# Fetching an expert block's rows in quarters of 512 bytes and transposing them on VectorE, in a fused attention and expert layer on one Trainium2 core

## The reference

```python
# B=32 batches, S=256 positions, 512 channels, 16 heads of 32, 8 expert tiles
x = x + attention(layernorm(x), ctx, ctx, Wq, Wk, Wv, Wo, masks)   # softmax over 256 masked keys
idx = argmax(pe @ sign(tile_sigs).T, axis=-1)                      # one expert for each position s
h   = layernorm(x)
x   = x + (h[b, s] @ W[idx[s]].T + b[idx[s]])                      # each row uses its position's expert
```

## Time and profile before

| | |
|---|---|
| median of 3 runs | 952.63 us (950.9 to 953.97) |
| the profiled execution, its own time | 953.35 us |
| its span, first to last instruction | 951.4 us |
| TensorE busy | 908.4 us (95%) |
| VectorE, GpSimd, ScalarE busy | 735.2, 567.1, 383.9 us |
| mean granted TensorE clock | 0.981 of 2.4 GHz |

### The profile page before, as it was taken

The page is one execution under the profiler, slowest core; times in us unless marked ns, Lnnn a source line. Parts: engine busy times, 40 slices in busy tenths (PEclk is TensorE's granted clock), DMA queues, the critical chain, the costliest instruction groups (busy, mean ns, idle before and its releaser), DMA issues.

```text
span 951.4 us, 16646 instructions
## 1 busy us (share of the span) xinstructions
PE 908.4 (95%) x5696; PEld 729.2 (77%) x5697; DVE 735.2 (77%) x1097; ACT 383.9 (40%) x697; POOL 567.1 (60%) x763
## 2 busy tenths in 40 slices
PE   5899999999999999999999999999739999999997
PEld 4687887887888788788878878887627888888885
DVE  5988867777776877877787787779758777777775
ACT  5554444454544445454444545444451111111110
POOL 3855746465574646557464654743645777777773
PEclk9999999999999999999999999999878999999999
DMA  9613133131313314131331313113643544444551
GB/s 336 225 72 102 56 113 91 60 121 46 104 53 113 101 53 117 45 110 48 113 102 56 113 45 113 52 51 117 224 142 112 158 161 162 163 158 159 162 164 50
DMA packets 48876, 108.10 MB, mean 114 GB/s; under 512 B 10496, under 2 KB 15136, under 8 KB 46624
## 3 DMA queue, kind: packets, MB, share of 16 engines
q1 hardware_dynamic: 37216, 71.70, 23.7%
q0 software_dynamic: 11200, 35.21, 11.6%
q10 hardware_dynamic: 384, 0.21, 0.1%
HBM read 73.47 MB, written 35.19 MB: 114 GB/s over the span
## 4 chain that ended last, share of the span: by engine, by line
PE 91%; DVE 3%; POOL 2%; DMA 1%; issue 1%; ACT 0%; SPq 0%; DVEq 0%; POOLq 0%
PE pS L1358 27%; PE pA L1652 21%; PE pA L1358 20%; PE pS L1416 7%; PE pA L1439 7%; PE pT L1427 6%; PE pT L1632 3%; PE pS L1384 1%; DMA x_scratch<-y 1%; POOL xt_lo L982 1%; POOL wo_lo L1030 0%; DMA wk_raw<-in_wk 0%; DMA xg<-x_scratch,gather_rows 0%; PE pT L1463 0%; DVE early L1312 0%
## 5 line engine op out<-in xcount | busy, mean ns | idle before, releaser
L1652 PE MATMUL pA<-wf_hl,x_hi 128*128 x560 | 183.3, 409 | 1.9 <-DVE x_lo L1586 1.9
L1203 DVE TENSOR_TENSOR s<-pS,bias 128x1024 f32<-128x1024 f32 x64 | 78.0, 1219 | 100.3 <-PE pS L1416 100.3
L998 POOL COPY y<-y_mom 128x1 f32<-128x1 f32 x64 | 12.9, 202 | 238.5 <-DVE y_mom L1242 238.5
L1015 POOL TENSOR_TENSOR s<-s,row 128x1024 f32<-128x1024 f32 x64 | 122.0, 1906 | 11.5 <-DVE row L1223 11.5
L1119 ACT CAST ot_hi<-pA 128x512 fp32r<-128x512 f32 x64 | 37.6, 588 | 222.6 <-PE pA L1439 222.6
L1546 POOL DMA_INDIRECT out_dram<-y,scatter_rows x70 | 94.1, 1344 | 54.4 <-DVE y L1594 52.8
L1565 ACT CAST x_hi<-pT 128x512 fp32r<-128x512 f32 x70 | 41.1, 587 | 191.0 <-PE pT L1632 159.1
L1652 PEld LDWEIGHTS pA<-wf_hl,x_hi 128*128 128x128 f32 x560 | 101.1, 191 | 21.2 <-issue 2.3
L1358 PE MATMUL pA<-wo_hi,ot_hi 128*128 128x512 f32 x256 | 109.2, 426 | 4.5 <-DVE ot_lo L1227 4.5
L1652 PE MATMUL pA<-wf_hl,x_lo 128*128 x280 | 111.5, 398 | 0.0
L1358 PE MATMUL pS<-xt_hi,wq_hi 128*128 128x512 f32 x256 | 105.6, 413 | 3.9 <-DVE wq_lo L1262 2.3
(11 more groups left out here) (124 smaller groups left out, 1898.9 us busy)
## 6 DMA issues: line engine op xcount, KB each, us to landing
x_scratch<-y SPq DMA_DIRECT2D x64, 257.0 KB, 3.0
xt_raw<-in_x_t SPq DMA_DIRECT2D x16, 1024.0 KB, 6.2
x<-in_x SPq DMA_DIRECT2D x64, 256.0 KB, 2.6
wf_hl<-in_wf SPq DMA_DIRECT2D x8, 1024.0 KB, 8.8
ctx_raw<-in_ctx_t SPq DMA_DIRECT2D x32, 128.0 KB, 3.1
bias_all<-in_bf SPq DMA_DIRECT2D x1, 2048.0 KB, 10.8
mask_early<-in_mask SPq DMA_DIRECT2D x1, 1536.0 KB, 11.6
xg<-x_scratch,gather_rows POOLq DMA_INDIRECT x70
```

What stands on the lines that cost most here:

```text
L1015: pool.tensor_tensor(p, p, h.row[:, t % h.c, 3, :].unsqueeze(2).broadcast_to([P, H, BK]), ALU.mult)\
L1203: dve.tensor_tensor(h.s_sb[:, t % h.c, :].rearrange("p (h k) -> p h k", h=H), pS[:, 0, :].rearrange("p (h k) -> p h k", h=H), h.bias[:, t ...
L1652: mm = pe.matmul(pA[:, r % 2, :], a[:, c * P:(c + 1) * P], w, start=(c == 0 and m == 0), stop=(c == KC - 1 and m == 2))
```

## The change

- Attention stores two things for each tile instead of one. `y_biased`, 128 rows of 2048 bytes: y plus the bias of its position's expert, by a GpSimd addition (`add_bias`). `y_normal`: the normalised rows, by a ScalarE activation (`y_normalise`), stored into a scratch `x_quarters` in which each quarter row (128 channels, 512 bytes) is a piece of its own.
- The two halves of the positions have their bias rows in `bias_at`, filled in the prologue by two indirect DMAs on GpSimd's queue, ahead of the low part of Wo. `bias_all` and its load go.
- In the expert stage GpSimd gathers only the biased rows. SyncE fetches the normalised ones, with one `value_load` and one DMA of 128 x 512 bytes for each of the block's four positions: 280 of each.
- These land with a quarter of the channels in each group of 32 partitions, so VectorE's transpose, which works in squares of 32x32, gives what the product needs (the expert weights' rows are reordered on the way in). TensorE's four transposes, VectorE's normalisation, its bias addition and its `value_load` go. The low part is now made from an SBUF tile and not from PSUM.

```diff
+        y_rows = nc.dram_tensor("y_scratch", (B * S, DM), F32, kind="Internal").ap()
+        x_quarters = nc.dram_tensor("x_scratch", (KC * B, S, P), F32, kind="Internal").ap()
...
+        def store_rows(sp, rows, batch, half, ring):
+            sp.dma_start(y_rows[rows, :], y_biased[:, ring, :]).then_inc(y_stored[ring], 16)
+            dst = x_quarters.rearrange("(i b) s f -> b s i f", i=KC)
+            sp.dma_start(dst[batch, half * P:(half + 1) * P] if isinstance(batch, int) else
+                         dst[batch, half * P:(half + 1) * P].rearrange("a s i f -> (a s) i f"),
+                         y_normal[:, ring, :].rearrange("p (i f) -> p i f", i=KC)).then_inc(y_stored[ring], 16)
...
             rstd(1)
+            pool.wait_ge(rv, MATCHED + 1)
+            for n in range(2):
+                pool.indirect_dma_start(bias_at[:, n, :], None, bf,
+                                        bass.IndirectOffsetOnAxis(ap=expert_at[:, n:n + 1], axis=0)).then_inc(bias_loaded, 16)
             pool.wait_ge(w_hi_ready["o"], 1)
...
+            def add_bias(t):
+                wait(pool, y_stored[t % 2], 32 * (t // 2))
+                pool.tensor_tensor(y_biased[:, t % 2, :], y_sb[:, t % 2, 0:DM], bias_at[:, t % 2, :], ALU.add)\
+                    .then_inc(y_biased_ready, 1)
...
+            def y_normalise(t):
+                y = y_sb[:, t % 2, :]
+                act.wait_ge(y_ready, t + 1)
+                wait(act, y_stored[t % 2], 32 * (t // 2))
+                act.activation(y_normal[:, t % 2, :], y[:, 0:DM], ACT.Identity, bias=y[:, DM:DM + 1],
+                               scale=y[:, DM + 1:DM + 2]).then_inc(y_normal_ready, 1)
...
+        def experts_sync(sp):
+            def gather_quarters(j):
+                r = j % R
+                wait(sp, x2t_ready, j + 1 - R)
+                for n in range(PB):
+                    s = sp.value_load(gather_rows[n * B:n * B + 1, j:j + 1], min_val=0, max_val=S - 1)
+                    sp.dma_start(xq[:, r, n * P:(n + 1) * P],
+                                 x_quarters[:, bass.ds(s, 1), :].rearrange("p a f -> p (a f)")).then_inc(quartered[r], 16)
+
+            for j in range(NR):
+                gather_quarters(j)
...
-                pool.indirect_dma_start(xg[:, r, :], None, x1,
+                pool.indirect_dma_start(yg[:, r, :], None, y_rows,
...
-                act.wait_ge(x2t_done, j + 1)
+                act.wait_ge(x2t_ready, j + 1)
                 wait(act, f_done, j - 1)
-                act.copy(x2_hi[:, j % 2, :], pT[:, j % 2, :]).then_inc(x2_hi_ready, 1)
+                act.copy(x2_hi[:, j % 2, :], x2t[:, j % 2, :]).then_inc(x2_hi_ready, 1)
...
+            def transpose(j):
                 r = j % R
-                wait(dve, x2t_done, j - 1)
-                dve.wait_ge(gathered[r], 16 * (j // R) + 16)
-                dve.tensor_scalar(xn2[:, j % 2, :], xg[:, r, 0:DM], xg[:, r, DM:DM + 1], xg[:, r, DM + 1:DM + 2],
-                                  ALU.subtract, ALU.mult).then_inc(xn2_ready, 1)
+                dve.wait_ge(quartered[r], 16 * PB * (j // R) + 16 * PB)
+                wait(dve, x2_lo_ready, j - 1)
+                dve.transpose(x2t[:, j % 2, :].rearrange("p (c g b) -> p c g b", c=KC, g=PB),
+                              xq[:, r, :].rearrange("p (g c a) -> p c g a", g=PB, c=KC)).then_inc(x2t_ready, 1)
...
             def body(k, n):
-                first = isinstance(k, int) and R * k + n == 0
-                if first:
-                    transpose(k, n + 1)
-                if is_block(k, n):
-                    e = expert(k, n)
-                if is_block(k, n + 1) and not first:
-                    transpose(k, n + 1)
-                if is_block(k, n):
-                    product(k, n, e)
+                product(k, n, expert(k, n))
```

More of the change, by code:

```diff
@@ L282, in kernel_program @@
         wf_loaded = [sem(f"wf_loaded_{t}") for t in range(NE)]
-        wf_hi_ready = [sem(f"wf_hi_ready_{t}") for t in range(NE)]
+        wf_hi_ready = sem("wf_hi_ready")
+        HIGH_ORDER = (0, 1, 2, 4, 5, 6, 7, 3)
         wf_lo_pool = sem("wf_lo_pool")
@@ L1057, in tiles @@
                 y_rstd(h.tiles - 2)
+                add_bias(h.tiles - 2)
                 y_rstd(h.tiles - 1)
+                add_bias(h.tiles - 1)
             return tiles
@@ L1182, in tiles @@
                         q_copy(g + 2, 0)
+                    if t >= 2:
+                        y_normalise(t - 2)
                     if t == h.tiles - 2:
                         expert_high(act, 1)
-                for t in (4, 5, 6, 7, 3):
+                y_normalise(h.tiles - 2)
+                expert_high(act, 4)
+                y_normalise(h.tiles - 1)
+                for t in (5, 6, 7, 3):
                     expert_high(act, t)
@@ L1522, in kernel_program @@
         y2 = sb("y2", [P, 3, DM])
-        xb_ready = sem("xb_ready")
         gathered = [sem(f"gathered_{r}") for r in range(R)]
-        xn2_ready = sem("xn2_ready")
-        x2t_done = sem("x2t_done")
+        quartered = [sem(f"quartered_{r}") for r in range(R)]
+        x2t_ready = sem("x2t_ready")
         x2_hi_ready = sem("x2_hi_ready")
@@ L1531, in kernel_program @@
         y2_ready = sem("y2_ready")
-        scattered = [sem(f"scattered_{r}") for r in range(R)]
+        scattered = [sem(f"scattered_{r}") for r in range(3)]
+        def experts_sync(sp):
[8 more added lines that the diff above has]
+                gather_quarters(j)
         def experts_gpsimd(pool):
@@ L1610, in experts_vector @@
                 if j + 2 < NR:
-                    normalise(j + 2)
+                    transpose(j + 2)
                 if j == 0:
@@ L1615, in experts_vector @@
                 finish(j)
-                if j + 1 < NR:
-                    add_bias(j + 1)
         def experts_tensor(pe):
             def at(k, n):
-                return R * k + n, n % R, k + n // R
-            def is_block(k, n):
-                return not isinstance(k, int) or 0 <= R * k + n < NR
-            def transpose(k, n):
-                j, r, turn = at(k, n)
-                pe.wait_ge(xn2_ready, j + 1)
-                wait(pe, x2_lo_ready, j - 1)
-                for c in range(KC):
-                    mm = pe.transpose(pT[:, r % 2, c * P:(c + 1) * P], xn2[:, r % 2, c * P:(c + 1) * P], ident[:])
-                mm.then_inc(x2t_done, 1)
+                return R * k + n, n % R
             def expert(k, n):
-                j, r, turn = at(k, n)
+                j, r = at(k, n)
                 e = pe.value_load(expert_of[0:1, bass.ds(j, 1)], min_val=0, max_val=NE - 1)
@@ L1672, in experts_tensor @@
                     body(k, n)
-            for n in range(NR + 1 - R * turns):
+            for n in range(NR - R * turns):
                 body(turns, n)
```

123 lines of the change are left out of this document (66 added, 57 removed).

## The result

The changed kernel takes 1090.91 us (median of 4, 1090.76 to 1091.67), the kernel before 952.98 us beside it: a ratio of 1.1452, 95% interval 1.1432 to 1.1472, so 14.5% slower. The forecast was 1069 us with a range of 1008 to 1125. The profiled execution has a span of 1089.9 us, against 951.4 before.

The account below looks back on a forecast made before the run. TensorE was taken to bound both stages, with SyncE pacing the changed expert stage: quarters start at 710.5, plus 342.3 us to the last issue at 1052.8, then the tail, a span of 1067.4; forecast 1069 us, range 1008 to 1125.

Parts of the forecast that it names:

- SyncE paces the stage: Expert stage: SyncE's loads and issues take 4.89 us per block (3.97 to 6.7), above the product's 2.80; chance 0.82.
- the rival with the DMA engines as the bound: Expert stage: DMA engines need 4.9 us per block, 1070 us in all, with a DMA share near 1; chance 0.04.
- 1.21 us for a quarter: Expert stage: SyncE's register load, bounds check, address, DMA issue and gaps for one position, between 0.98 and 1.66 us.
- TensorE's 30.8 us: Expert stage: 70 blocks without four transposes of 0.44 us in all save TensorE 30.8 us, which turn into idle time.
- TensorE busy for about 57%: Expert stage: TensorE works 2.80 us of each 4.89 us block, with a granted clock below 1.
- Start of the quarters, 710.5: Change-over to the expert stage: SyncE's quarters start at 710.5 us, 4.2 us later than the gathers' start before.
- The prologue: Two bias gathers in GpSimd's chain ahead of Wo's low part cost 3.2 us on the path, between 2.3 and 4.7.
- Attention, costed at nothing: Attention: GpSimd's addition, ScalarE's activation and the second store hide under TensorE's 100%; without that cover 98 us.
- The change-over: Attention to expert stage: stores start at about 705 us, behind the last expert's weights, which load 3.2 us later.
- The tail: After the last issue: landing 2.6, transpose 0.8, rounding 0.6, low part 0.9, product 2.8, then 6.9 us to the end.
- The clock: Expert stage: TensorE's clock goes up and down at little cost; rival staying at 1.2 GHz, about 1086 us, chance 0.04.
- The DMA share: Expert stage: a DMA share of about 0.5 to 0.6, against 0.49 before.

Follow-up runs that it names:

- e1: The changed kernel without its 280 register loads, SyncE issuing the same 280 DMAs from constant positions (rows not the block's): 933.63 us, one run.
- e3: The changed kernel with quarters 2 and 3 of each block fetched by ScalarE's queue, five blocks ahead: 937.57 us, ratio 0.984 to the kernel before.
- e9: The changed kernel with every one of SyncE's register loads done twice, 280 more loads: 1242.23 us, one run.
- e14: The changed kernel with register loads without bounds, so no FUSED_REGOPS and SEQ_ASSERT: 1005.95 us.
- e7_before_bias: The kernel before plus only the two bias gathers ahead of Wo's low part and the instruction making their indices: 960.66 us, ratio 1.0081.
- e10: e3 with the last expert's weights loaded ahead of tile 62's store and GpSimd finishing tiles 62 and 63 first: 967.57 us, ratio 1.0153.
- e8: e34 with the change-over's order as in e10, and ScalarE issuing two blocks before its first rounding, not five: 959.16 us, ratio 1.0055.
- e34: e3 with the two bias gathers moved behind the first softmax division in GpSimd's prologue: 963.79 us, ratio 1.0103.
- e5: The changed kernel without register loads, one DMA of 128 x 2048 bytes per block from constant positions (rows not the block's): 930.81 us, one run.

## Why the prediction was right, point by point

- *SyncE paces the stage: right, and shown.* With the loads gone (e1) or shared by two queues (e3) TensorE is at 100%; with entries added (e9) or taken away (e14) the time follows them. The time alone would not have told: the rival with the DMA engines as the bound, forecast at 1070 us, lay at the same place, and e1 and e3 exclude it.
- *1.21 us for a quarter: measured 1.262.* FUSED_REGOPS was 0.15 instead of 0.19, SEQ_ASSERT 0.02 for 0.03, the DMA issue 0.34 for 0.38. The address took 0.04 and a MOVE that was not foreseen 0.03, together 0.07 for 0.06. The five entries beside the load make 0.58 us, six gaps of 0.03 to 0.05 us about 0.25, which leaves some 0.43 us for the load instead of 0.35: near the end of the stage it alternates between 0.27 and 0.46, and a few loads take longer. Errors in both directions partly cancel, which is luck: 353.4 us instead of 342.3, +11.1.
- *TensorE's 30.8 us: nothing of it is seen*, as predicted. In e3, where it can show, a block takes 2.71 instead of 3.24 us, yet the kernel gains only 15 us, since the stage starts later (first product at 735.4 instead of 716.15).
- *TensorE busy for about 57%: wrong in size.* It was 72 to 77%. 239 matmuls in 71.7 us are 3.6 us for a product, not 2.8, at a granted clock of 0.84 to 0.86. Under 5.05 us for a block that costs nothing.
- *Transpose on VectorE: 0.71 us* for the guess of 0.70 between 0.60 and 2.4.
- *Start of the quarters, 710.5: the worst term, measured 722.8.* It is 16.5 us later than the gathers' start before, instead of 4.2.
  - The prologue gave 7.0 us (52.38 to 59.39) for 3.2. The step that failed: the gathers were costed only for what is queued behind them on GpSimd, not for what GpSimd's chain then does to VectorE. (The upper end of 4.7 us is not what its own terms give either: 0.91 + 2.26 + 0.30 + 0.98 = 4.45.) The prediction cited the Trainium skill's page "SBUF — State Buffer" (section "SBUF: two separate sides") for GpSimd being locked out by VectorE. The same section says that whichever of the two starts first keeps the ports, and the other waits. Here the shift started 0.28 us ahead of Wo's low part, and Wo's took its usual 4.6 us; it was the shift that waited, for 7.8 us more than before. The measurement decides.
  - Attention, costed at nothing, gave 2.1 us (the last piece of 24 matmuls starts at 642.30 instead of 633.21, 9.1 later). All of it is in the query projections: in each group a single piece of 12 matmuls takes 2.99 instead of 2.93 us, and two others are 0.03 and 0.06 us longer, while the rest is the same. In e7_before_bias, whose tiles have none of the new work, only 0.4 us of it is seen. Why they are longer was not tested.
  - The change-over: the last store was issued 4.1 us later still, of which 2.0 were in the sum (one more step and the bias addition 1.6, the second issue 0.4). The prediction let the load of the last expert's weights come 3.2 us later; it came 14.6 us later, behind the stores of tile 62, and the last store right behind it took 8.98 us to land. In the prediction 5.3 us lay between that store's issue and the start. In e10, where this load goes first, the last store is issued as late as here (713.33), yet the quarters start at 718.0, 4.8 us earlier: so it is the load just ahead of the store that holds up its landing.
  - Beyond what was in the sum this is 3.8 us in the prologue, 2.1 in attention, 2.1 to the store's issue, 3.7 in its landing and 0.5 until the first load: 12.2 of the 12.3 us.
- *The tail* took 1089.9 - 1076.3 = 13.6 us instead of 14.6.
- *Sum:* 1067.4 + 12.3 + 11.1 - 1.0 = 1089.8, against a span of 1089.9.
- *The clock* went up and down, 0.84 to 0.86 on average, and cost next to nothing, as said; in the chain that ended last only the second last product, 4.61 us, shows it.
- *The DMA share* of 0.5 was as foreseen, but there is less room than it seemed: at TensorE's full pace it is 0.95.

The change-over's reordering (e8) gave 4.6 us over e34, and moving the gathers 8.5 us over after. A kernel with e3's pace and both savings would be an estimated 937.6 - 8.5 - 4.6 = 925 us, if they add; both shorten the landing of the last store, so they may not in full. The stalls kept every attempt from it. The best that was measured is e3.

## What to carry to other kernels

Before giving a sequencer dynamic addresses, count its entries: the load of a position, its bounds check, the address and the DMA issue took 1.26 us here, and four of them outweighed a product of 2.8 us. Share such issues between two queues (and look whether they then run without the stalls that five of six kernels had here), drop bounds that nobody needs, and look at what stands ahead of the stage. When instructions are put into a full prologue, look for what the work behind them now runs beside, not only for what it delays.

## What was not expected of the hardware

- Bounds on a register load cost 0.32 us of SyncE's time per quarter, a quarter of the whole.
- VectorE's shift, with two SBUF inputs, took 10.8 us beside GpSimd's chain of low parts (after; 10.7 in e7), up to the end of the chain, and 2.99 us in the kernel before, where it got in after the first of them.
- Cutting the same bytes into 512-byte instead of 2048-byte pieces cost only 3.5 to 5.7 ns of one DMA engine for each additional packet, at 288 GB/s and a share of 0.95 (e1 against e5).
- With dynamic DMAs on two queues, the sequencers of SyncE and TensorE (in one of them ScalarE's too) crawled together at 0.7 us per step in five kernels of six.
